# VectorE's order of work in a relational graph kernel: finish and gather index ahead of the weights

## The reference

```python
h = jnp.maximum(_layernorm(x, axis=-1), 0.0)
dots = jnp.sum((h[src] @ tokeys.T) * relations[rel] * (h[src] @ toqueries.T), axis=1) / e
values = jnp.exp(dots)
fr = src + n * rel
rowsum = segment_sum(values, fr)
msgs = (values / rowsum[fr])[:, None] * h[dst]
output = segment_sum(msgs, fr).reshape(r, n, e)
weights = einsum('rb,bij->rij', comps, bases_w)
out = x + relu(einsum('rij,rnj->ni', weights, output))
```

## Time and profile before

| what | value |
|---|---|
| median of 3 runs | 3504.29 us (3500.42 to 3507.05) |
| the profiled execution | 3509.78 us, its span 3508.1 us |
| PE, PEld busy | 1627.4 us (46%), 1346.8 us (38%) |
| DVE busy | 1562.7 us (45%) |
| POOL busy | 1737.2 us (50%) |
| ACT busy | 469.9 us (13%) |
| mean granted TensorE clock | 0.673 |

### The profile page before, as it was taken

One profiled execution on the slowest core, in us unless ns is written; L12 is line 12 of the kernel. 1 busy time (PEld: TensorE's weight loads), 2 busy tenths in 40 slices (PEclk: granted clock), 3 DMA queues, 4 the chain that ended last, 5 costly groups with the idle time before them and its releaser, 6 DMA issues.

```text
span 3508.1 us, 34157 instructions
## 1 busy us (share of the span) xinstructions
PE 1627.4 (46%) x11900; PEld 1346.8 (38%) x11901; DVE 1562.7 (45%) x2015; ACT 469.9 (13%) x946; POOL 1737.2 (50%) x1730
## 2 busy tenths in 40 slices
PE   3999999950332433324333243332333334333333
PEld 2666666640332333324233242332323334233333
DVE  6999999951333232332323333233232323323232
ACT  1334333310000000000000000000000000000000
POOL 1233323245555565555655556555464655656553
PEclk8888888865666666666666666656656666665666
DMA  3212112111111111111111111111111111111111
GB/s 90 86 73 85 74 75 84 73 54 41 37 40 42 38 45 38 41 42 37 45 37 40 42 38 45 38 41 42 36 45 36 44 38 38 44 37 44 37 41 27
DMA packets 71666, 169.05 MB, mean 48 GB/s; under 512 B 29075, under 2 KB 37468, under 8 KB 65217
## 3 DMA queue, kind: packets, MB, share of 16 engines
q0 software_dynamic: 52704, 106.67, 11.8%
q1 hardware_dynamic: 18940, 62.10, 4.8%
HBM read 112.09 MB, written 56.56 MB: 48 GB/s over the span
## 4 chain that ended last, share of the span: by engine, by line
PE 43%; issue 32%; another core or an unknown queue 12%; DVE 8%; ACT 3%; DMA 1%; DVEq 0%; ACTq 0%; POOL 0%; SPq 0%; POOLq 0%
PE bank L1034 20%; PE bank L931 8%; PE bank L946 6%; DVE arena L649 3%; ACT pay_all L858 2%; DVE bank L642 2%; PE bank L1013 2%; PE bank L1006 1%; PE bank L1022 1%; PE bank L910 1%; PE bank L911 1%; DMA stage<-in_edge_type 1%; PE bank L938 1%; PE bank L939 1%
## 5 line engine op out<-in xcount | busy, mean ns | idle before, releaser
L390 POOL DMA_INDIRECT arena<-Z_messages,IDX x1593 | 1506.8, 946 | 1193.3 <-DVE IDX L611 722.3
L1034 PE MATMUL bank<-arena 128*128 128x128 f32 x3528 | 701.6, 365 | 1539.2 <-issue 1022.6
L1034 PEld LDWEIGHTS bank<-arena 128*128 128x128 f32 x3528 | 647.0, 275 | 1592.5 <-issue 1311.7
L858 ACT COPY pay_all<-bank 128x1024 bf16<-128x1024 bf16 (+1 forms) x245 | 208.2, 946 | 2526.9 <-PE bank L1013 2463.6
L640 DVE TENSOR_TENSOR M<-bank,OHR 128x432 f32<-128x432 f32 x196 | 119.0, 607 | 898.8 <-remote 870.4
L621 DVE TENSOR_SCALAR WC<-bank 128x16 f32<-128x16 f32 x49 | 8.6, 175 | 903.6 <-PE bank L1006 903.6
L347 POOL DMA_INDIRECT bucket_streams<-REC,IDXW x50 | 72.3, 1445 | 461.0 <-ACT REC L809 422.7
L931 PE MATMUL bank<-pay_all,stage 125*128 125x98 f16 x1600 | 296.1, 360 | 0.6 <-ACT PFS L789 0.5
L931 PEld LDWEIGHTS bank<-pay_all,stage 125*128 125x128 f16 x1600 | 236.5, 149 | 51.1 <-issue 0.8
L649 DVE TENSOR_TENSOR arena<-stage,bank 128x4608 f32<-128x4608 bf16 x49 | 242.7, 4953 | 1.7
L604 DVE TENSOR_TENSOR stage<-bank,NLF 128x4608 bf16<-128x4608 f32 x49 | 242.5, 4948 | 0.0
(11 more groups left out here) (150 smaller groups left out, 1327.6 us busy)
## 6 DMA issues: line engine op xcount, KB each, us to landing
Z_messages<-stage SPq DMA_DIRECT2D x48, 1024.0 KB, 3.9
arena<-Z_messages,IDX POOLq DMA_INDIRECT x1593
out<-O SPq DMA_DIRECT2D x48, 64.0 KB, 1.6
arena<-in_L_gnn_bases_w SPq DMA_DIRECT2D x1, 1024.0 KB, 24.1
RL<-bucket_streams SPq DMA_DIRECT2D x49, 18.0 KB
Z_messages<-stage SPq DMA_DIRECT2D x1, 848.0 KB
bucket_streams<-REC,IDXW POOLq DMA_INDIRECT x50, 3.0
stage<-in_src SPq DMA_DIRECT2D x1, 781.2 KB
```

Of the source, the lines that this page charges most:

```text
L390: g.indirect_dma_start(Gbuf[par][:, k, :], None, Z, bass.IndirectOffsetOnAxis(IDX[par][:, k:k + 1], 0))\
L858: a.copy(OHT[:, 8 * k:8 * k + n, :].rearrange("p k e -> p (k e)"), bank[TPB[k]][:, :].bitcast(BF16)[:, 0:n * P]).then_inc(s["oht"], 1)
L1034: mm = t_.matmul(bank[2][:, 0:EMB], OW[:, k, :], Gbuf[par][:, k, :], start=(k == 0), stop=(k == G - 1))
```

## The change

In DVE's step, `weights(b)` moves behind `finish(b-1)` and `gather_index(b+1)`. Nothing is added or removed, and no other engine's code changes.

```diff
                     if dyn(b) or b + 1 < NB:
                         tables(b + 1, 1 - par)
-                    if dyn(b) or b < NB:
-                        weights(b, par)
                     if dyn(b) or 1 <= b:
                         finish(b - 1, 1 - par)
                     if dyn(b) or b + 1 < NB:
                         gather_index(b + 1, 1 - par)
                     if dyn(b) or b < NB:
+                        weights(b, par)
                         edge_weights(b, par)
                         weighted_onehot(b, par)
```

## The result

The changed kernel takes 4126.32 us (median of 4 runs, 4123.87 to 4128.85), the kernel before 3502.36 us beside it (3500.18 to 3507.05): ratio 1.178, 95% interval 1.1759 to 1.18, 624 us more. The profiled execution took 4123.87 us, its span is 4122.1 us, the mean granted clock 0.644.

A forecast was written before the change was run, and what follows sets the result against it. It took each bucket's period to end with the gather, beside which PE's matmuls finish late. L640 at +43.5, aggregate at +53.7 plus 9.9 us gave 63.6 against 55.1 us; 47 periods, +400 us: 3904 us, range 3375 to 4200.

The forecast's parts named there:

- The sign and the case: Whole kernel: slower, because the earlier gather overlaps PE's transposes; 3904 us, chance 0.54 for this case.
- Step 1: DVE and POOL: finish and index write no longer wait for the weights; gather starts at +1.3 instead of +4.05 us.
- Step 2: DVE: weights after finish and index write still start at about +0.93 us, at no cost.
- Step 3: PE: gather begins amid the transposes; ACT's copies come late, L640 idles near 40 us, 8.5 us more per period.
- my count of 64 matmuls: PE beside the gather: 27 transposes, 36 lookups and 1 turn must finish before L640 can start.
- my 42.2 us: Time from the gather's start to L640, taken as the middle of 40.6 to 43.8 us.
- the six matmuls beyond 58: PE's matmuls past the 58 done 35.4 us after the gather's start; they were to cost 5.2 to 8.4 us.
- The break-even of 56 matmuls: PE: no loss if L640 starts by +35.0 us, 33.7 us after the gather's start, at 0.87 us a matmul.
- My bound from above: L640 comes 10.5 us after the gather's last issue in every bucket: +818 us, 4322 us.
- Rows 4: Profile rows of the kernel's start, the one place showing a gather overlap the transposes; ACT started 35.4 us after it.
- the first rival: Gather pulled forward whole, transposes on time: each period 2.7 us shorter, 127 us in all, 3377 us; chance 0.32.
- The other rival: PE's lateness is not the gather's doing, so nothing changes: 3504 us; chance 0.14 together with the slack case.

The follow-up runs named there:

- e1b_finish_only: Kernel before with only finish moved ahead of the weights, the index write left behind them: 3479.27 us, ratio 0.999.
- e2b_index_only: Kernel before with only the index write moved ahead of the weights, finish left behind them: 4110.62 us, ratio 1.1807.
- e3b_late_lookups: Kernel before with six extra ACT copies, so the lookups start 8.7 us after the gather's start: 4207.01 us, ratio 1.2005.
- e6_half_gather: Changed kernel with one DMA for every 256 edges instead of 128, leaving out half of the gathered rows: 3018.98 us.
- e5_index_after_lookups: Kernel before with finish ahead of the weights and the index write held until the lookups are done: 3635.16 us, ratio 1.0376.
- e4b_index_mid: Kernel before with finish first and the index write between the fourth and fifth of the weights' eight links: 3427.15 us, ratio 0.9782.
- the first four runs: Finish alone, index write alone, late lookups, index write mid-weights, each against the kernel before on one chip: 2789.37 to 2789.67 us, ratios 0.9998 or 0.9999.
- r2_after: Changed kernel, unedited, run again beside the kernel before on another chip: 4120.05 us, ratio 1.1805.

## Why the prediction was right in direction and short in size

**The sign and the case** were right: the gather beside the transposes and lookups makes the bucket longer, and the period ends with an undisturbed aggregate.

**Step 1** held, 0.2 us later than I took. POOL starts at +1.50 (I took +1.3, bounded by +1.42, so just outside), because finish starts at +0.27 and not within 0.03 to 0.2; the index write follows at +0.48. `e1b_finish_only` and `e2b_index_only` show that only the index write acts.

**Step 2** held: L621 at +0.93, and the weights, done at +2.8 (2046.07 + 0.17), had over 7 us of cover, since the lookups waited for ACT until +10.15.

**Step 3** gave the right picture for a wrong reason. As stated, ACT's copies came late and L640's idle time was near 40 us (44.08). But my count of 64 matmuls since the gather's start does not set the release: `e3b_late_lookups` owes 37, as the kernel before does, and waits as long as the changed kernel. That my 42.2 us came near the measured 45.3 (32 DMAs) and 46.7 us (33) was luck: the six matmuls beyond 58 gave a sum of about the gather's own length. The statement "if L858 is on time and L640 is late all the same, the lateness comes from the gather's age at the lookups and not from the transposes' share" was put to the test by that run: L858 came on time, L640 late all the same, so it went against the count. The break-even of 56 matmuls falls with it.

**The size.** I put L640 at +43.5 and the aggregate at 9.9 us; the traces have +47 and 10 to 10.5. The period came to 68.2 instead of 63.6 us, and 47 x 4.6 = 216 us is what 3904 us lacks of the measured time, up to some 6 us. The mis-sized term is the six matmuls beyond 58, "5.2 to 8.4 us". The release is set by the gather: 32.5 DMAs x 1.41 = 45.8 us from its start at +1.5. My bound from above, last issue plus 10.5 us, had the right form and 5 us too much; it came from a place where a second gather had begun behind the first. Rows 4 fit the same rate: 65 DMAs in the two gathers, and L640 91.5 us after the first issue (867.20 against 775.66), 1.41 us a DMA. The distance from the last issue's end to L640 grows with the number of DMAs because 1.41 us is more than the 1.25 us of an issue: 3.2 us for 16, 5.7 for 32, 10.5 for 65. What I read there as 1.40 us a matmul was this pace of the gathers.

What the runs put in its place is one sum: gather's start + 1.41 us a DMA + what PE and DVE still owe then. Only the price of a DMA was found from runs; the last term is read off each timeline and not forecast. After: 1.5 + 45.8 + 10.2 (L640 to aggregate) + 10.5 = 68.0, measured 68.2. `e6_half_gather`: 1.4 + 16.5 x 1.41 + 20.7 = 45.4, and its two aggregates above end 45.0 us apart. `e5_index_after_lookups`: 10.9 + 33 x 1.41 = 57.4, with nearly nothing owed; its aggregate ends at +58.2. `e4b_index_mid`: 3.0 + 45.1 = 48.1, and its 52.1 us leave 4.0 for the last matmuls. The change moved the first term by -2.6 us and the last from about 5 us (54.35 - 4.05 - 45.1) to 20.7 us, because the lookups no longer got through ahead of the backlog. So the first rival, the gather pulled forward whole, is partly real: `e4b_index_mid` takes 1.05 us of its 2.7 us and leaves the transposes untouched, and gains 76 us; 47 x 1.05 = 49 of them are the gather's start, the rest is in the last term. The other rival, that the gather is not what makes PE late, is out by two runs: with no gather yet the lookups are released at once (`e5_index_after_lookups`), and with half of it they are about a third as late (`e6_half_gather`, 12.7 against 35.1 us).

**The rule that spoke against.** The Trainium skill, "SBUF — State Buffer", section "Who interferes with whom", says "PE and ACT never wait on anyone". On the chip of the first four runs the trace agrees (L640 0.13 us behind the lookups). On the others PE's results are 35.1 us late beside the gather, so whoever plans by the rule there goes wrong, and the measurement decides. The page speaks of ports of SBUF, and no run shows whether one of these is what holds PE.

**Open.** Why lookups 3.2 us into the gather are 3.4 to 15.9 us late before (12.0 to 12.5 in half of the buckets), at 4.3 us 5.2 to 5.4 us in 45 of 47 buckets, and at 8.6 us held to the end; this is not monotone. `e1b_finish_only` does not settle it: its output store is early, as in `e4b_index_mid`, its lookups come 3.5 to 3.6 us in and are 5.9 to 18.3 us late. Between 4.3 and 7.8 us nothing was tried; at 7.8 us, where 15 buckets of `r2_after` have them, they are held to the end too (L640 5.3 to 5.6 us after the last issue's end in 11 of them, 3.3 to 4.7 in four). So the runs show that the changed kernel loses because its lookups are held to the gather's end, and that the earlier index write alone brings this about, but not the rule by which they are held. What holds PE's results, and why one chip lacks it, is open too, and so is whether recording the trace has a part in it. The loading of code is not it: the two instruction queues of the profile moved 22 packets in the whole execution before and 23 after.

## What to carry to other kernels

Starting a transfer sooner is only worth its lead if the engines beside it still get their own work released. Find in the timeline which short steps run just behind the transfer's start, and pull it forward in small steps, with a measurement at each. Here the end of the transposes was the place: a start at +3.0 us gained 2% where +1.5 us lost 18%, and +10.9, behind the lookups, lost 4%. Measure on more than one chip; `e4b_index_mid` is 2% faster where PE falls behind, and takes the same time (ratio 0.9999) where it doesn't.

## What was not expected of the hardware

- The same kernel takes 2790 us on one chip and 3484 to 3503 us (medians) on two others, at the same 946 ns a gather issue. The only difference seen is when PE's results are released beside a gather.
- PE's stamps show the lookups done at 2055.25 and the instruction that waits for them starts at 2090.32. On such a chip the stamps of matmuls beside a gather do not tell when others can use the results; the reader's start does, and the semaphore event just before it (2090.20).
- While it is late, PE's aggregate goes on in steps: matmuls 0.70, 1.40, 2.10 or 2.80 us apart. In `e5_index_after_lookups`:

```profile
2076.75 0.37 PE L1036 MATMUL bank<-arena 128*128 128x128 f32 x1 [2.43 <-issue]
2079.55 0.37 PE L1036 MATMUL bank<-arena 128*128 128x128 f32 x1 [2.43 <-issue]
2081.65 0.37 PE L1036 MATMUL bank<-arena 128*128 128x128 f32 x1 [1.73 <-issue]
2084.45 0.37 PE L1036 MATMUL bank<-arena 128*128 128x128 f32 x1 [2.43 <-issue]
```

0.70 us is half of the 1.41 us a DMA found above.

- It takes a while to show in the stamps: in the bucket of `e5_index_after_lookups` shown above, the first 49 matmuls of the aggregate ran at full pace, 7.12 us for them, though they began 9.3 us into the gather.
